# Another order of the steps of a 32-batch layer on one core, with steps of one TensorE tiling side by side

## The reference

```python
# 1. gated cross attention with random features (causal), m = 64 features per head
q, k, v = heads(layernorm(x)), heads(ctx), heads(ctx)
q_prime = exp(q*s @ F) + 1e-4                       # (256, 64) per head
k_prime = exp(k*s @ F - |k*s|^2/2 - max) + 1e-4
for t in range(256):                                # causal prefix sums
    S += k_prime[t][:, None] * v[t];  Z += k_prime[t]
    out[t] = (q_prime[t] @ S) / (q_prime[t] @ Z)
x = x + tanh(g_xattn) * out
# 2. gated block
h = rmsnorm(layernorm(x), gamma1)
q = h @ Wq + bq;  k, v = split(((h @ Wdown + bdown) @ Wup + bup))
att = softmax(q[t] @ k[t].T / 4)                    # 16 x 16, heads against heads, per token
y = layernorm(x) + (att @ v) @ Wo + bo
h2 = rmsnorm(y, gamma2);  gate = softmax(h2 @ Wg + bg)      # 8 experts
x = x + tanh(g_ffn) * (y + sum_e gate[e] * (h2 @ We[e]))
```

## Time and profile before

| | |
|---|---|
| median of 3 runs | 1334.33 us (1331.05 to 1337.19) |
| profiled execution | 1344.52 us |
| its span, first to last instruction | 1342.8 us |
| mean granted clock of PE | 0.982 |
| busy: PE, PE's loads | 1255.5 us (93%), 975.1 us (73%) |
| busy: DVE, ACT, POOL | 936.9 us (70%), 755.1 us (56%), 559.2 us (42%) |

### The profile page before, as it was taken

How to read it: one execution, slowest core, us unless ns; L and a number is a source line. 1 busy time by engine, 2 the same in 40 slices (tenths; PEclk the granted TensorE clock), 3 DMA queues, 4 the chain that set the end, 5 groups by cost and what they waited for, 6 DMA issues and landing times.

```text
span 1342.8 us, 55815 instructions
## 1 busy us (share of the span) xinstructions
PE 1255.5 (93%) x25344; PEld 975.1 (73%) x25344; DVE 936.9 (70%) x2166; ACT 755.1 (56%) x1502; POOL 559.2 (42%) x873
## 2 busy tenths in 40 slices
PE   0568999999999999999999999999999999999997
PEld 0347777777777777777777777777777777777775
DVE  5465677677777677766777777777777777777665
ACT  5366655565555565654556556555665555566431
POOL 0254345343434443443444444454444434444421
PEclk9987999999999999998999999999999999999999
DMA  8300000000000000000000000000000000000000
GB/s 283 106 18 18 19 26 26 27 3 26 27 26 26 27 18 11 26 27 26 26 27 8 21 26 27 26 26 27 26 2 27 26 26 26 27 26 3 10 19 16
DMA packets 40221, 40.72 MB, mean 30 GB/s; under 512 B 4144, under 2 KB 39728, under 8 KB 39984
## 3 DMA queue, kind: packets, MB, share of 16 engines
q1 hardware_dynamic: 38896, 37.11, 8.9%
q10 hardware_dynamic: 1088, 0.04, 0.1%
HBM read 28.75 MB, written 8.39 MB: 28 GB/s over the span
## 4 chain that ended last, share of the span: by engine, by line
PE 92%; DVE 3%; issue 2%; POOL 1%; DMA 1%; SPq 1%; ACT 1%; DVEq 0%
PE ps L1593 15%; PE ps L1595 12%; PE ps L1594 12%; PE ps L1624 10%; PE ps L1639 8%; PE ps L1666 7%; PE ps L1658 6%; PE ps L1632 5%; PE ps L1587 4%; PE ps L1609 4%; PE ps L1649 3%; DVE hk L1367 1%; PE ps L1875 1%; DMA x_in<-in_x 1%; SPq L319 1%
## 5 line engine op out<-in xcount | busy, mean ns | idle before, releaser
L1047 DVE SCALAR_TENSOR_TENSOR z<-ps,gate,z 128x256 f32<-128x256 f32 x512 | 247.4, 483 | 143.8 <-PE ps L1595 133.3
L1593 PE MATMUL ps<-we_hi,h_hi 128*128 128x512 f32 x512 | 226.2, 442 | 3.3 <-issue 1.2
L1595 PE MATMUL ps<-we_hi,h_lo 128*128 128x512 f32 x512 | 204.9, 400 | 0.0
L1594 PE MATMUL ps<-we_lo,h_hi 128*128 128x512 f32 x512 | 204.1, 399 | 0.0
L1624 PE MATMUL ps<-qf,kf 64*128 64x256 f32 x1024 | 148.9, 410 | 4.0 <-POOL qf L373 4.0
L1593 PEld LDWEIGHTS ps<-we_hi,h_hi 128*128 128x128 f32 x512 | 97.6, 191 | 33.4 <-issue 12.2
L1666 PEld LDWEIGHTS ps<-v_t,p_t 32*32 32x32 f32 x8192 | 84.3, 107 | 48.7 <-issue 47.8
L495 POOL TENSOR_TENSOR x<-o_x,x_in 128x512 f32<-128x512 f32 x32 | 41.1, 1285 | 188.3 <-DVE o_x L1274 188.3
L1624 PEld LDWEIGHTS ps<-qf,kf 64*128 64x128 f32 x1024 | 90.5, 190 | 34.4 <-issue 23.0
L1595 PEld LDWEIGHTS ps<-we_hi,h_lo 128*128 128x128 f32 x512 | 97.9, 191 | 23.2
L1639 PE MATMUL ps<-att,v 128*32 128x256 f32 (+1 forms) x2048 | 111.9, 334 | 1.2 <-DVE att L1205 0.6
(11 more groups left out here) (210 smaller groups left out, 3076.4 us busy)
## 6 DMA issues: line engine op xcount, KB each, us to landing
x_in<-in_x SPq DMA_DIRECT2D x32, 256.0 KB, 3.5
c_in<-in_ctx SPq DMA_DIRECT2D x32, 256.0 KB, 3.2
c_chunk<-in_ctx SPq DMA_DIRECT2D x16, 512.0 KB, 7.4
out<-z SPq DMA_DIRECT2D x32, 256.0 KB, 2.6
stage<-in_L_ffn_We SPq DMA_DIRECT2D x2, 1024.0 KB, 9.8
stage_q<-in_L_ffn_Wq SPq DMA_DIRECT2D x1, 256.0 KB, 6.4
stage_u<-in_L_ffn_Wup SPq DMA_DIRECT2D x2, 128.0 KB, 5.4
stage_b<-in_L_ffn_bup SPq DMA_DIRECT2D x1, 256.0 KB, 6.6
```

The lines of the kernel that those rows point to most:

```text
L1047: return dve.scalar_tensor_tensor(out=z[e % 2][:, t, :], in0=ps[:, bank, ex % 2 * D:(ex % 2 + 1) * D], scalar=gate[:, t, ex:ex + 1], in1=z ...
L1593: pe.matmul(out, a_hi(c), b_hi(c), start=(c == 0), stop=False)
L1594: pe.matmul(out, a_hi(c), b_lo(c), start=False, stop=False)
L1595: last = pe.matmul(out, a_lo(c), b_hi(c), start=False, stop=(c == C - 1))
```

## The change

No step is added, removed or altered inside; the number of matmuls, evictions and bytes is the same. What changes is the order of the steps in `slot` on PE, DVE, ACT and POOL, the batch distances (loads and the first stage run at n + 2 instead of n + 1, the key products at n + 1 instead of n), the steps ahead of the loop, the PSUM banks, the waits that follow from these, and the grouping of semaphores. On PE, steps of one kind of tiling stand next to each other more often.

```diff
-BANK = dict(x000=5, x001=0, x010=0, x011=3, y00=7, y01=4, av0=7, x100=6, x101=2, x110=5, x111=4, y10=7, y11=6,
+BANK = dict(x000=7, x001=0, x010=4, x011=5, y00=3, y01=2, av0=3, x100=0, x101=4, x110=7, x111=5, y10=5, y11=6,
...
-            mm03=6, mm10=3, mm11=3, mm12=7, mm13=2)
+            dn=2, qq=5, kv0=2, kv1=4, s=1, pv=4, otr=7, o=7, h20=6, h21=7, g=6, mm00=6, mm01=7, mm02=3,
+            mm03=0, mm10=2, mm11=1, mm12=1, mm13=7)
...
             def load_x_(q):
-                if 2 <= q <= 4:
+                if q >= 2:
                     sp.wait_ge(*at("x1", q - 2))
...
             def X00_(p):
-                if p >= 3:
+                if p >= 4:
+                    pe.wait_ge(*at("a01", p - 4))
...
+                if p >= 6:
                     pe.wait_ge(*at("pq1", p))
```

More of the change, by code:

```diff
@@ L248, in build @@
[L248 to L257, removed]
@@ L259, in build @@
+            signal("e_pe_b", "mm03 mm10 mm11 mm12 mm13"),
+            signal("e_dve", "ga gmax gm gsum grec gate a00_ a00 a01_ a01 a02_ a02"),
+            signal("e_dve_b", "a03_ a03 a10_ a10 a11_ a11 a12_ a12 a13_ a13"),
             signal("e_act", "gl gexp"),
@@ L334, in _ @@
                              we_d[:, c * P:(c + 1) * P, :].rearrange("e p f -> p e f")).then_inc(*we_in.up(0))
[L335 removed]
+            for n in range(-2, NB + 3):
                 slot(n)
@@ new lines, in x_normal, with nt0_ @@
+            @per_batch
+            def x_normal(q):
+                act.wait_ge(*at("q_r", q))
+                for t in range(T):
+                    last = act.activation(xn[:, t, :], x_in[q % 2][:, t, :], ACT.Identity, scale=rstd[:, t:t + 1], bias=shift[:, t:t + 1])
+                last.then_inc(*up("xn", q))
+            @per_batch
+            def nt0_(p):
+                if p in (0,) or p >= 5:
+                    act.wait_ge(*at("av1", p))
+                act.activation(nt[:, 0:2, :].rearrange("p a b -> p (a b)"), ps[:, BANK["av0"], :], ACT.Copy).then_inc(*up("nt0", p))
@@ L1035, in _ @@
+            eq1_(5)
+            eq3_(5)
+            k_high(5)
+            eq0_(5)
+            d_hi_(3)
+            ot_high(2)
+            eq2_(5)
+            nt1_(4)
+            ek0_(5)
+            ek1_(5)
+            ek3_(5)
+            q_apart(3)
+            ek2_(5)
+            y_normal(3)
+            sq_(2)
+            for n in range(-2, NB + 3):
                 slot(n)
@@ new lines, in h2_t1_, with mm11_ @@
+            @per_batch
+            def h2_t1_(f):
+                if f >= NB - 3:
+                    pe.wait_ge(*at("a01", f - 1))
+                for t in range(T):
+                    last = pe.transpose(ps[:, BANK["h21"], t * P:(t + 1) * P], h2n[:, t, 1 * P:2 * P], ident[:, :])
+                last.then_inc(*up("h2_t1", f))
+            @per_batch
+            def mm11_(e):
+                if e and e + 2 < NB:
+                    pe.wait_ge(*at("ssub", e + 2))
+                expert_products(e, 1, 1, BANK["mm11"]).then_inc(*up("mm11", e))
@@ L2116, in _ @@
+            pv3_(2)
+            mm00_(1)
+            keys_turned(5)
+            dn_(3)
+            qq_(3)
+            o_tr_(2)
+            kv0_(3)
+            kv1_(3)
+            av2_(4)
+            av3_(4)
+            fk_(5)
+            out_project(2)
+            nt_t_(4)
+            mm01_(1)
+            mm02_(1)
+            for n in range(-2, NB + 3):
                 slot(n)
```

2208 lines of the change are left out of this document (1242 added, 966 removed).

## The result

The change made the kernel a little slower: 1342.57 us against 1333.94 us (medians of 20 runs each), ratio 1.0061 with a 95% interval of 1.0043 to 1.0080. That lies inside the range of 1280 to 1360, on the other side from the forecast of 1310. The profiled execution took 1344.9 us, 2 us above its median, while the first profile of before was 10 us above its own.

A forecast was written before the change was run, and what follows sets the result against it. PE was taken as the bound: what it issues plus issue waits. Switches -54, pages +25 and clock +5 sum to -24 us, against the median of 1334.3 giving 1310 us; range 1280 to 1360 for 8 in 10 runs.

The forecast's parts named there:

- The base: In the steady part, PE's time is what it issues plus issue waits; no semaphore makes it wait in 29 batches.
- Rivals 3 and 4: X01, X11, av1 waits expose first loads, 1322, chance 0.08; X00 waits for DVE's a01 through shared bank 7, 1339, 0.10.
- Term 1: On PE, fewer changes of tiling save 1.9 us a batch, 28.5 batches' worth: -54 us.
- Term 2: Joined 32x32 steps use up 256-instruction pages before the next arrives: 1.39 us a batch against 14.6 us now, +25 us.
- Term 3: Long page waits, some 13 instead of 7, bring 3 or 4 more half-clock pieces on PE: +5 us.
- Rival 5: Every page wait slows PE's clock, each with a slow piece: +65 us, 1399 us; chance 0.02.
- Rival 1: Pages stay hidden, A is near 2.94, and the joints pay in full: 1282 us; chance 0.14.
- rival 2: Page waits of 1.5 to 2.5 us at s0 or pv0 halve the clock, A acts as 3.73: 1362 us; chance 0.16.
- 35 to 45 us of issue waits: Sign of being right: PE's issue waits three times as many, in L1870, L1878 and just behind.
- 37.5 us a batch: Sign of being right: average between two steady starts of s0, with 36.4 where no page waits.

The follow-up runs named there:

- before_again: The kernel before, unchanged, profiled a second time: span 1334.2 us, execution 1335.9 us.
- spread_v2: The changed kernel with its 32x32 steps apart again, pv0 moved ahead of g_ on PE and p_turned ahead of a10 on DVE: 1297.6 us, ratio 0.9754 to before.

## Why the prediction went wrong

**The base.** "PE's time is the sum of what it issues plus issue waits" held: one steady wait for another engine in 29 batches, as forecast. Rivals 3 and 4 fell with it (X01 starts 0.97 us behind X00, within the joint's price; X00 does not wait).

**Term 1, switches, was right in its mechanism**: -54 forecast, -54.9 by the table, which is the steady saving for 32 batches. That the two agree to a microsecond is luck: per batch the joints save 1.7 us and not 1.9, and the 28.5 batches' worth were 32.

**Term 2, pages, is the step that failed.** Place, period and mechanism were right: 256 instructions apart, in L1870, L1878 and just behind. The size was not: +25 forecast, +40 measured in the whole program. In the prediction's own measure (idle time + 0.19 per wait, steady part) it is 43.4 + 53 x 0.19 = 53.5 us, 1.84 a batch instead of 1.39. The failing choice was the allowance A (the time in which a page must not be used up) of 3.3 us, "about the middle" between 2.94 and 3.73. In the changed kernel's records, the first matmul behind a border with a wait mostly starts 3.3 to 3.8 us after the border before (3.73 in the fence above; a few are down to 1.5, some above 4). Its packet mostly starts 0.8 to 1.5 us after that earlier border, takes 0.9 to 1.4 us, and the matmul follows 1.2 to 1.6 us later. 3.3 is the low end of that, not its middle. The 2.94 was no bound at all: no score step waited in before, but a page can be ahead, and in the changed kernel two borders 1.3 us apart passed without a wait. A lower bound from "it did not wait here" holds only where the page was asked for at the last moment. Of the 178 pages of the steady part, 80 hold less than 3.3 us of work (natural time from border to border); 64 of these made PE wait by more than 0.1 us, with 3.5 us from border to matmul on average, and none of the other 98 did. The 52 pages of about 3 us cost 0.82 us a batch instead of 0.56, the 28 shorter ones 0.99 instead of 0.83: two waits a batch, each some 0.2 us longer than A = 3.3 gives.

Nor is one allowance for all pages enough. In the kernel before only 14 of 30 such pages made PE wait, and four of its waits of about a microsecond (300, 457, 657 and 1006 us; the first is in the earlier trace rows) stand behind pages that took 6.0 to 6.95 us, with packets that start only 3.4 to 4.4 us after the border. What sets the time at which a page is asked for stays open.

**Term 3, the clock: +5 forecast, +13 measured.** Half-clock stretches in the steady part are 58 us long against 20. One behind the wait at 442.17 us in the changed kernel, columns as in the earlier trace rows, and an expert step inside it:

```profile
442.70:446.10 3.40, 3.40 (x21) 2.79 (x19) 2.33 (x5) 0.50 (x1) 1.41 (x4) 0.50 0.02 5
```

```profile
445.18 0.63 PE L1807 MATMUL ps<-we_hi,h_lo 128*128 128x512 f32 x1
445.61 0.63 PE L1805 MATMUL ps<-we_hi,h_hi 128*128 128x512 f32 x1
```

The passes start 0.43 us apart instead of 0.23. Each of the 15 steady stretches begins in or within 2 us of a gap of 1.09 us or more from one matmul's start to the next (0.91 us of idle time), none at a shorter one; five more such gaps (230, 269, 401, 463 and 773 us) have none. In the kernel before the shortest such gap is 1.03 us, 0.84 idle, in the earlier trace rows. So the premise stood; but 18 waits lost a microsecond or more, not 13, and three in four drew the clock down. I had also counted the kernel before wrongly: a fifth stretch begins at 1123.4 us and the one at 614.8 is of double length, so five of its seven long waits had one, with 20.4 us together, not four. Rival 5 fell: about two waits a batch, and half a stretch. The Trainium skill, "TensorE: Matmul & The Clock Gate", "A second HAM failure mode: psum-queue depth-cycling", lets short idle times between groups of matmuls do this too; here none of the some thirty shorter waits of the changed kernel did.

**What the sum left out.** The start: the first matmul is queries_turned(0), at 12.3 us where before began at 6.9, +5.4, of which 2.9 came back in other waits. And the base of the comparison: I moved a difference of -24 from the profiled execution of before to the median of its runs, but that execution was slow through the very waits that the terms count. Against before_again (page waits 17.2, clock 16.3) both terms grow by 6 and 4 us. That is about the difference between +0.4 in the first pair of profiles and +8.6 in the medians.

**The rivals.** Rival 1 fell with the 53 waits. What happened lies between the forecast and rival 2 ("pages take it all back"): the pages and the clock do take it all back, but waits of 1.5 to 2.5 us, as rival 2 has them, are six of the 53; most are under a microsecond. I gave it 0.16, because I took the page to be early in front of both clusters. Two of my signs did not follow from my sum. The 35 to 45 us of issue waits came, 43.4, but 40 was the term's measure, with 0.19 per wait, in which 53.5 came. And 37.5 us a batch is too low for the sum, which gives 36.4 + 1.39 and some clock, 38 or more; measured are 38.9, and 36.56 without waits. A saving of 24 us left over from 54 and 30 was thin.

## What to carry to other kernels

Cheap instructions are not free where they come thick: in the changed kernel 64 of 80 pages of 256 PE instructions with less than 3.3 us of work made PE wait for the next (14 of 30 in the kernel before, 4 of 21 in spread_v2), and 15 of 20 gaps of 1.09 us or more had a stretch at half clock behind them. Look for issue waits a fixed number of instructions apart, and before you group small matmuls to save changes of tiling (0.14 to 0.20 us each), put the count of instructions beside the time they take; here the best order, spread_v2, joins what is slow and keeps most of the dense steps 1.6 to 3 us of other work apart, 2.5% faster than before, and 3.4% with its borders moved. When two orders differ by less than a per cent, move the borders by half a page and time both again.

## What was not expected of the hardware

- A semaphore instruction of PE on a value long reached takes 0.08 to 0.09 us: 128 of them are 9.9 to 11.7 us of idle time.
- Moving the borders by 128 instructions, with nothing else changed, takes the ratio to before from 1.0061 to 0.9942 in the changed kernel (12 us between the medians) and from 0.9754 to 0.9660 in spread_v2 (6 us between the medians, where the kernel before was 6 us slower in the second series). In both, 8 us of the profiled span are saved by batch 4.
- The same program has 2 to 10 us more or fewer page and clock losses from one execution to the next, with its natural batch within 0.06 us.
- Open: whether it is the number of instructions or the bytes that count, what sets the time at which a page is asked for, and why the borders' place matters so much at the start. None was tried further.
